# Fused two-layer attention on one core: the first head group's scores move one slot ahead, and GpSimd normalises the second input of each pair

## What is computed

```python
xn = layernorm(x, g_in);  q = xn @ Wq;  k, v = split(xn @ Wkv)
k, v = [null_k; k], [null_v; v]
sim = q @ k.T + [null_bias | bias[h]];  sim = where(causal | padding, -max, sim)
out = layernorm((softmax(sim) @ v) @ Wo, g_out)
x = x + out            # layer 0, then the same with layer 1
```

## Time and profile before

| what | value |
|---|---|
| median of three runs | 2237.0 us |
| the profiled execution's own time, and its span | 2237.55 us, 2235.8 us |
| PE busy | 2077.9 us, 93% of the span |
| DVE, ACT, POOL busy | 1625.1, 1562.1, 1028.6 us |
| mean granted clock of TensorE | 0.989 of full speed |
| chain that ended last | PE 62%, DVE 16%, DMA 6%, issue 5%, ACT 4% |

### The profile page before, as it was taken

One profiled execution on the slowest core, in us unless ns is written; L12 is line 12 of the kernel. 1 busy time (PEld: TensorE's weight loads), 2 busy tenths in 40 slices (PEclk: granted clock), 3 DMA queues, 4 the chain that ended last, 5 costly groups with the idle time before them and its releaser, 6 DMA issues.

```text
span 2235.8 us, 72261 instructions
## 1 busy us (share of the span) xinstructions
PE 2077.9 (93%) x26395; PEld 1859.0 (83%) x26395; DVE 1625.1 (73%) x3422; ACT 1562.1 (70%) x6241; POOL 1028.6 (46%) x1510
## 2 busy tenths in 40 slices
PE   4799999999999999999999999999999999999987
PEld 4788888888888888888888888888888888888876
DVE  5677777777777777777777777777777777777775
ACT  4567777777777677776777776676677677677775
POOL 3444444444544544544444444444444444444453
PEclk8899999999999999999999999999999999999998
DMA  8112222212222212222222221122221122221111
GB/s 257 41 55 61 70 61 61 67 55 60 72 61 61 67 55 60 72 61 61 62 59 61 72 61 56 58 68 59 69 64 55 57 68 61 63 68 58 59 59 45
DMA packets 183034, 147.47 MB, mean 66 GB/s; under 512 B 121440, under 2 KB 125616, under 8 KB 182992
## 3 DMA queue, kind: packets, MB, share of 16 engines
q1 hardware_dynamic: 181248, 145.77, 21.8%
q0 software_dynamic: 688, 1.14, 0.3%
q10 hardware_dynamic: 1056, 0.00, 0.0%
HBM read 98.56 MB, written 37.77 MB: 61 GB/s over the span
## 4 chain that ended last, share of the span: by engine, by line
PE 62%; DVE 16%; DMA 6%; issue 5%; ACT 4%; SPq 3%; POOL 2%; DVEq 0%; POOLq 0%; ACTq 0%
PE psum L708 21%; PE psum L581 15%; PE psum L615 11%; DVE probs L1128 6%; PE psum L690 6%; PE psum L673 4%; DMA xa<-in_x_dram 4%; ACT probs L896 4%; DVE neg_max L1134 2%; POOL probs L1466 2%; SPq L443 2%; PE psum L592 2%; DVE o_lo L1151 2%; DMA v_kept<-v_diff 2%; DVE bn_in L1068 2%
## 5 line engine op out<-in xcount | busy, mean ns | idle before, releaser
L896 ACT ACTIVATE probs<-probs,neg_max 128x129 f32<-128x129 f32 (+3 forms) x2048 | 712.7, 352 | 66.7 <-DVE neg_max L1134 66.7
L1456 POOL TENSOR_TENSOR masked_bias<-bias,pad_neg 128x516 f32<-128x516 f32 (+3 forms) x512 | 403.9, 821 | 220.1 <-DVE probs L1128 214.1
L1466 POOL TENSOR_TENSOR probs<-probs,den_inv 128x512 f32<-128x512 f32 (+3 forms) x512 | 368.0, 740 | 214.2 <-DVE den_inv L1139 214.1
L1478 POOL TENSOR_TENSOR y_out<-y_out,res 128x512 f32<-128x512 f32 x128 | 164.7, 1287 | 538.0 <-ACT y_out L860 538.0
L896 ACT ACTIVATION_READ_ACCUMULATOR probs<-probs,neg_max 128x1 f32 x2048 | 386.7, 189 | 0.0
L1144 DVE STREAM_TRANSPOSE probs_t<-probs 128x512 f32<-128x512 f32 (+3 forms) x512 | 230.0, 487 | 138.3 <-POOL probs L1466 137.2
L708 PE MATMUL psum<-wo_hi,o_hi 128*128 128x512 f32 x1024 | 275.3, 411 | 19.9 <-DVE probs L1128 18.5
L1128 DVE TENSOR_TENSOR probs<-psum,masked_bias 128x648 f32<-128x648 f32 x256 | 201.5, 828 | 118.3 <-PE psum L673 118.0
L708 PE MATMUL psum<-wo_hi,o_lo 128*128 128x512 f32 x1024 | 264.9, 400 | 21.0 <-DVE o_lo L1151 21.0
L708 PE MATMUL psum<-wo_lo,o_hi 128*128 128x512 f32 x1024 | 260.6, 396 | 0.0
L708 PEld LDWEIGHTS psum<-wo_hi,o_lo 128*128 128x128 f32 x1024 | 187.5, 188 | 77.1 <-DVE o_lo L1151 25.9
(11 more groups left out here) (133 smaller groups left out, 3986.8 us busy)
## 6 DMA issues: line engine op xcount, KB each, us to landing
res<-in_x_dram SPq DMA_DIRECT2D x64, 256.0 KB, 2.7
v_rep<-v_kept SPq DMA_DIRECT2D x512, 32.0 KB, 1.8
x_of<-y_out SPq DMA_DIRECT2D x64, 256.0 KB, 2.1
res<-x_of SPq DMA_DIRECT2D x64, 256.0 KB, 2.7
out_dram<-y_out SPq DMA_DIRECT2D x64, 256.0 KB, 2.1
xa<-in_x_dram SPq DMA_DIRECT2D x63, 256.0 KB, 2.7
xa<-x_of SPq DMA_DIRECT2D x63, 256.0 KB, 2.9
q_aside<-qp SPq DMA_DIRECT2D x32, 256.0 KB, 3.1
```

Of the source, the lines that this page charges most:

```text
L896: x_ = nc.scalar.activation(s, s, ACT.Exp, bias=neg_max[:, b, n:n + 1], accum_out=den[:, b, n:n + 1])
L1456: m = nc.gpsimd.tensor_tensor(block(masked_bias, b), block(bias[u.layer], b), pad_neg[u.layer][:, 0:WIDTH[b]].unsqueeze(1).to_broadcast([P ...
L1466: m = nc.gpsimd.tensor_tensor(some, some, den_inv[:, b, :].unsqueeze(2).to_broadcast([P, 4, n]), ALU.mult)
L1478: nc.gpsimd.tensor_tensor(y_out[:, :], y_out[:, :], res[:, :], ALU.add).then_inc(out_done, 1)
```

## The change

`scores(then, 0)` and `add_bias(then, 0)` are now called at the end of a slot for the unit of the next one; a slot begins with `scores(u, 1)` and `add_bias(u, 1)`. In `first` and `second` the call on PE stands ahead of `values`, in `late` between the first two and the last two of its four blocks of keys, so `values` takes a list of blocks. `project_out` waits for each half of its operand apart. `add_bias(u, 0)` waits for `turn` of the unit before, since it writes `probs` earlier. In `first`, the normalisation of `w.odd` goes from DVE to the start of POOL's slot, ACT calls `split_x(w.even)` ahead of `rstd_of_input(w.odd)`, and DVE's two `split_o` go ahead of two of the four `row_max`; in `second` one `split_o` does so. The diff, without the start-up slots:

```diff
@@ tensor @@
-            def values(u):
+            def values(u, blocks):
...
-                for k in range(BLOCKS):
+                for k in blocks:
...
             def project_out(u, p, now=None):
+                arrived = {0: o_hi_done, 2: o_lo_done}
                 if p == 0:
-                    for b in range(2):
-                        wait(pe, o_hi_done[b], u.done)
...
                 for k in range(PAIRS):
                     j = k // 2 + 4 * (k % 2)
+                    if p in arrived and k % 4 == 0:
+                        wait(pe, arrived[p][k // 4], u.done)
...
             def first(u, v, w, n, then):
-                scores(u, 0)
                 scores(u, 1)
...
                 project_pair(w, 0, (0, 1, 2, 3), u)
-                values(u)
+                scores(then, 0)
+                values(u, range(BLOCKS))
...
             def second(u, v, w, n, then):
-                scores(u, 0)
                 scores(u, 1)
...
                 project_pair(w, 1, (3,), u)
+                scores(then, 0)
                 wait(pe, pair_v_ready, w.pdone * 2)
-                values(u)
+                values(u, range(BLOCKS))
...
             def late(u, v, w, n, loads, then, pairs_done):
                 if u:
-                    scores(u, 0)
                     scores(u, 1)
...
-                    values(u)
+                    values(u, range(2))
+                if then:
+                    scores(then, 0)
+                if u:
+                    values(u, range(2, BLOCKS))
@@ scalar @@
             def first(u, v, w, n, then):
+                split_x(w.even)
                 rstd_of_input(w.odd)
-                split_x(w.even)
...
@@ vector @@
             def add_bias(u, c):
                 if c == 0:
+                    for g in range(len(GROUPS)):
+                        wait(dve, turned[g], u.prev)
...
             def first(u, v, w, n, then):
                 input_statistics(w.odd)
-                add_bias(u, 0)
                 add_bias(u, 1)
                 row_max(u, 3)
-                normalise(w.odd)
                 row_max(u, 1)
                 split_x(w.even)
+                split_o(v, 0)
+                split_o(v, 1)
                 row_max(u, 2)
                 row_max(u, 0)
-                split_o(v, 0)
-                split_o(v, 1)
...
                 normalise(n)
+                add_bias(then, 0)
...
@@ gpsimd @@
+            def normalise(u):
+                wait_apart(pool, xt_done, u.xprev, pool_passed)
+                wait_apart(pool, rstd_in_done, u.xdone, pool_passed)
+                nc.gpsimd.tensor_scalar(xn[:, :], xa[:, :], mv_in[:, 0:1], rstd_in[:, 0:1], ALU.subtract, ALU.mult).then_inc(xn_done, 1)
...
             def first(u, v, w, n, then):
+                normalise(w.odd)
                 mask_bias(then)
```

More of the change, by code:

```diff
@@ L675, in scores @@
                 m.then_inc(scores_done[c], 1)
-            def values(u):
+            def values(u, blocks):
                 n, filled = side(u)
[L679 to L684, removed]
+                if 0 in blocks:
+                    wait(pe, v_rep_loaded[n], filled * 16 * 4)
+                    wait(pe, o_lo_done[1], u.prev)
+                    for g in range(len(GROUPS)):
+                        wait(pe, turned[g], u.done)
+                    if not isinstance(u.done, int):
+                        pe.sem_inc(pe_passed, 1)
                 p_t = probs_t[:, :, :, :, :].rearrange("p (c e) k b i -> p c e k b i", e=2)
-                for k in range(BLOCKS):
+                for k in blocks:
                     for e in range(2):
@@ L701, in project_out @@
                         wait(pe, biased[0], now.done)
-                if p == 2:
-                    for b in range(2):
-                        wait(pe, o_lo_done[b], u.done)
                 os, ws = ((o_hi, wo_hi), (o_hi, wo_lo), (o_lo, wo_hi))[p]
@@ L761, in first0 @@
                 transpose_diagonals(u)
[L762 removed]
+                values(u, range(BLOCKS))
+                pe.wait_ge(diag_computed, 1)
+                scores(then, 0)
             def second0(u, v, w, n, then):
[L765 to L766 removed]
                 scores(u, 1)
```

6 lines of the change are left out of this document (3 added, 3 removed).

## The result

The changed kernel took 2403.62 us (median of 4 runs, 2401.88 to 2407.14) against 2237.57 us for the kernel before in the same measurement: 1.0744 times as long, interval 1.0725 to 1.0762. The profiled execution took 2404.85 us, its span 2403.1 us. The forecast was 2195. The mean granted clock fell from 0.989 to 0.958.

A forecast was written before the change was run, and what follows sets the result against it. PE was taken as the bound, with 95 us of nothing in its pipeline. From 2237.55 us, 57.0 + 28.1 - 33.9 - 12.2 + 4 = 43 us were taken off, giving 2195 us, range 2178 to 2226.

The forecast's parts named there:

- no DMA is added: Remark on the rest of the change: no further DMA, SP's waits met earlier; no time was put on it.
- POOL's normalisation: In `first`, normalising the second input on POOL takes 0.71 us, between 0.34 and 1.29, and the move costs nothing.
- The cover: In `first`, PE's work up to the second transposes hides the normalisation on POOL; 0.3 us is left at `values`.
- the rival of POOL's queue: POOL's in-order queue becomes the bound in `first`: up to 0.7 us a round, 20 us, so 2215 us; chance 0.15.
- Scores a slot ahead: In each slot, transposes and output projection no longer wait for DVE's bias addition: 57.0 us won over the loop.
- The low part in `first`: PE's wait for the output's low part from DVE goes: 0.97 us a round, 28.1 us won.
- The new wait in `second`: PE waits for ACT's copy of the last query tile ahead of the next unit's scores: 1.17 us a round, 33.9 lost.
- Changes of tile size: Six more switches of PE's matmul tile size a round, at 0.07 us each: 12.2 us lost.
- The rival of the drains: Gaps behind `scores(u, 1)` are mostly 64x64 to 128x128 tile changes, so the 57.0 us stay: 2251 us; chance 0.10.
- Waits for each half: In `second`, the projection waits for ACT's first half of the high part: 0.1 us at most, counted as nothing.
- Start and end: Outside the loop's rounds, shorter waits for the bias give 4 us, between 0 and 12.7.

The follow-up runs named there:

- the shifted kernel: The changed kernel with 188 more instructions (376 already met waits) in PE's queue ahead of the loop: 2242.51 us, ratio 1.0018.
- the shift by 30: The kernel before with 30 more instructions (60 already met waits) in PE's queue ahead of the loop: 2296.83 us.
- in three portions: The changed kernel with the 188 added instructions split 70, 58 and 60, each ahead of a long start-up wait of PE: 2233.02 us, ratio 0.9981.

## Why the prediction was wrong

- **The step that failed: "no DMA is added".** The sum priced what each instruction does and gave nothing to where the instructions lie. Moving `scores(then, 0)` ahead of the loop shifted PE's loop by 60 instructions, and 252 loads of code were added, on a queue that the argument never looked at. That is 170.6 us, more than all its terms together, and no rival had it. The wait is in the trace of the changed kernel, 4.72 us in the return shown, and nine blocks are loaded for each return. Going back as such costs nothing like it: the kernel before goes back 1713 instructions, nearly seven blocks by the estimate, with no load after its first round, and its "issue" there is 0.9 us at the longest.
- **POOL's normalisation, the second step that failed.** Its price was continued straight from forms of 6 and 128 columns to 0.71 us, with 1.29 as the upper bound; it measured 2.08. The cover "ends where the normalisation takes over 1.0 us" fits (8.0 us ahead of the second transposes and 24.0 ahead of `values` over 29 rounds, so 1.1 a round, were exposed), and the rival of POOL's queue was right in kind and place. Its price was not: 37.1 us instead of 20. The same form on DVE takes 0.54 us at the shortest, 0.92 in the median of the kernel before, and 1.24 in the earlier trace rows.
- **Scores a slot ahead** was right: the waits for the bias, 57.0 us, are gone.
- **The low part in `first`** was right: the wait is gone, and 0.2 us is left of it in the kernel before with the normalisation alone on POOL. There the third product starts 0.36 us after the second transposes (1064.66 to 1065.02), 1.38 before. But with the normalisation back on DVE it starts after 0.35 (1057.08 to 1057.43), so the move that cost 37.1 us was not needed for it.
- **The new wait in `second`** was right: 1.17 us forecast, 1.30 measured, 37.6 us instead of 33.9.
- **Changes of tile size**: from the start of `values` to the transposes, less the wait, took 2.96 us before (1009.99 to 1013.35, less 0.40). At the end of a `late` of the shifted kernel (its PE rows above) the same work, with two more changes, runs from 1065.20 to 1068.34, so 3.14. That is 0.09 us for a change, an estimate: 15.7 us instead of 12.2. The rival of the drains is out: the gaps went with the bias.
- **Waits for each half**: put at nothing, 0.2 us a round, 6.2 us.
- **Left out of the reading**: 95 us of PE's idle time in the stretch (1955.00 less 1860.22) were spoken of and 78 named. Another row was there, the first scores of each round:

```profile
PE psum L673 <- issue: 14.2, 29, 0.9
```

- It is gone in the changed order (0.2 us with the normalisation on DVE); which part takes it away, no run isolates.
- **Start and end**: the loop's first matmul came at 112.5 instead of 116.5 us, 4 us as forecast; what lies behind the 29 rounds takes 1.4 us more.

With these sizes, and the normalisation on DVE, the terms are 57.0 + 28.1 + 14.2 - 37.6 - 6.2 - 15.7 + 4 = 43.8 us, less 11.2 for the 188 instructions at the start (123.7 against 112.5 us): 32.6. Measured were 2237.0 - 2205.4 = 31.6: the 29 rounds took 41.6 us less, what lies ahead of them 9.1 and what lies behind 0.9 more. So some 43 us are there once POOL's price and the code's place are taken away; the first was put too low, the second never counted. That this meets the forecast's 43 so closely is luck in part: the 14.2 us that nobody forecast make up for 13.4 us by which the copy, the high part and the changes of tile cost more.

## What to carry to other kernels

Before moving work across a loop's start, look at the instruction queue's row and at PE's "issue" at the return: this loop of 1713 instructions passed from no loads in its later rounds to nine blocks a round by a shift of 60 instructions, and then a good change measures as a bad one. Shift the loop's code by a harmless block before judging the order. An operation moved to another engine is priced from that engine's rows of the same length and type, and where there is none, by a run of that operation alone.

## What the runs showed of the hardware

A loop of 1713 instructions is loaded once where it starts at instruction 1532 or 1788 of PE's queue (26 and 27 blocks in the whole run) and every round where it starts at 1592 (279); at 1562 it changes from round to round (117). So the place decides, and 256 instructions more change nothing of it. That the loop lies over seven blocks in the one case and eight in the other, and that the engine holds seven, is not shown: it needs blocks that begin 31 to 82 instructions ahead of the program. A return that misses costs 4.6 to 5.0 us by the rounds of the shift by 30, and the round behind it 1.2 to 2.2 more. After the pause the granted clock is 0.51 over 5.65 us in the stretch shown, and 1.00 ahead of it. Met waits of PE, two to an instruction, cost 0.06 to 0.08 us an instruction where they stand together (11.2 us for 188, 20.6 for 256), and little where PE would wait anyway: in three portions the 188 cost 1.8 us at the start (114.3 against 112.5).
